# First loads and splits in parts, zero products beside them, and VectorE's small steps in shorter strings: a two-layer kernel on one core

## The reference

```python
x = layernorm(x + L0_attn(x))   # linear attention, 16 heads of 128, 4 key/value heads
x = layernorm(x + L0_ffn(x))    # a gate picks one of 8 small updates per token
x = layernorm(x + L1_attn(x))   # softmax attention, 16 heads of 16
x = layernorm(x + L1_ffn(x))    # 8 experts, the two best per token

# L0_attn
sq, sk = elu(q) + 1, elu(k) + 1
kv = einsum('bhsd,bhse->bhde', sk, v)
out = einsum('bhsd,bhde->bhse', sq, kv) / (einsum('bhsd,bhd->bhs', sq, sk.sum(2)) + 1e-6)
# L0_ffn: gate = sigmoid(slope * (score - center)); argmax and max over the 8
# L1_ffn: scores = softmax(x @ G); top 2 of 8 weigh the experts
```

## Time and profile before

| what | value |
|---|---|
| time, median of 3 runs | 769.73 us (767.15 to 775.13) |
| the profiled execution's own time | 768.48 us |
| its span, first to last instruction | 766.7 us |
| mean granted TensorE clock | 0.934 |
| PE busy | 700.3 us, 91% |
| DVE busy | 509.6 us, 66% |
| ACT busy | 405.0 us, 53% |
| POOL busy | 110.4 us, 14% |

### The profile page before, as it was taken

The page is one execution under the profiler, slowest core; times in us unless marked ns, Lnnn a source line. Parts: engine busy times, 40 slices in busy tenths (PEclk is TensorE's granted clock), DMA queues, the critical chain, the costliest instruction groups (busy, mean ns, idle before and its releaser), DMA issues.

```text
span 766.7 us, 11317 instructions
## 1 busy us (share of the span) xinstructions
PE 700.3 (91%) x4028; PEld 481.7 (63%) x4028; DVE 509.6 (66%) x1125; ACT 405.0 (53%) x746; POOL 110.4 (14%) x107
## 2 busy tenths in 40 slices
PE   4799999999999999997899988999999899999674
PEld 3677988798878887895344534555565455455463
DVE  2657755775577666767778777868779786772343
ACT  2376536643674377453037745764647565656222
POOL 0401321132203322243002010200001000000000
PEclk9899999999999999998559969998999999999868
DMA  8300000010000020008704810373006700000000
GB/s 340 128 0 2 28 1 1 2 31 14 0 0 0 11 77 1 4 1 103 100 2 55 98 15 2 44 90 36 2 2 77 89 30 2 1 2 29 28 1 27
DMA packets 13596, 28.30 MB, mean 37 GB/s; under 512 B 2596, under 2 KB 3436, under 8 KB 13036
## 3 DMA queue, kind: packets, MB, share of 16 engines
q1 hardware_dynamic: 13548, 27.68, 19.6%
HBM read 12.60 MB, written 2.10 MB: 19 GB/s over the span
## 4 chain that ended last, share of the span: by engine, by line
PE 74%; DVE 14%; ACT 5%; issue 3%; DMA 2%; POOL 1%; ACTq 0%; DVEq 0%; POOLq 0%
PE bank_y L391 11%; PE bank_q L332 10%; PE bank_st L1134 9%; PE bank_c L1147 6%; PE bank_a L296 6%; DVE nmax L1699 5%; PE side L1206 4%; PE bank_a L362 3%; PE side L1082 3%; PE bank_s L1113 3%; PE side L1237 2%; PE bank_a L308 2%; PE bank_n L347 2%; PE bank_q L374 2%; PE side L1166 2%
## 5 line engine op out<-in xcount | busy, mean ns | idle before, releaser
L1699 DVE TENSOR_REDUCE nmax<-bank_s 128x1 f32<-128x512 f32 x256 | 164.5, 684 | 62.8 <-PE bank_s L1113 62.2
L1460 ACT ACTIVATE shared<-bank_st 128x512 f32<-128x512 f32 x256 | 139.2, 596 | 78.4 <-PE bank_st L1134 77.8
L1113 PE MATMUL bank_s<-ks,qs 48*128 48x512 f32 x256 | 117.7, 524 | 10.4 <-DVE nmax L1699 8.6
L1134 PE MATMUL bank_st<-qs,ks 50*128 50x512 f32 x256 | 104.8, 480 | 5.6 <-ACT shared L1460 5.4
L578 DVE SCALAR_TENSOR_TENSOR sq<-bank_q,bq,eq 128x512 f32<-128x512 f32 x64 | 47.6, 743 | 52.2 <-ACT eq L473 52.2
L1134 PEld LDWEIGHTS bank_st<-qs,ks 50*128 50x128 f32 x256 | 42.6, 197 | 54.6 <-issue 28.0
L391 PE MATMUL bank_y<-m_hi,s_lo 128*128 128x256 f32 x256 | 73.3, 286 | 3.2 <-POOL s_lo L248 3.1
L1147 PE MATMUL bank_c<-shared,v 128*32 128x512 f32 x512 | 73.5, 648 | 0.9 <-ACT shared L1460 0.9
L391 PE MATMUL bank_y<-m_lo,s_hi 128*128 128x256 f32 x256 | 72.1, 282 | 0.0
L391 PE MATMUL bank_y<-m_hi,s_hi 128*128 128x256 f32 x256 | 72.1, 282 | 0.0
L248 POOL TENSOR_TENSOR s_lo<-sq,s_hi 128x512 fp32r<-128x512 f32 x32 | 42.8, 1339 | 189.5 <-ACT s_hi L478 189.5
(11 more groups left out here) (251 smaller groups left out, 1329.8 us busy)
## 6 DMA issues: line engine op xcount, KB each, us to landing
qs<-qk_hi SPq DMA_DIRECT2D x16, 256.0 KB, 5.9
ks<-qk_hi SPq DMA_DIRECT2D x16, 256.0 KB, 10.2
xT<-in_xT SPq DMA_DIRECT2D x4, 512.0 KB, 5.3
sq<-in_wqT SPq DMA_DIRECT2D x2, 1024.0 KB, 9.2
wo<-in_woT SPq DMA_DIRECT2D x1, 2048.0 KB, 12.9
xs<-in_x SPq DMA_DIRECT2D x1, 2048.0 KB, 17.8
qs<-qk_lo SPq DMA_DIRECT2D x8, 256.0 KB, 7.9
ks<-qk_lo SPq DMA_DIRECT2D x8, 256.0 KB, 10.9
```

The lines of the kernel that those rows point to most:

```text
L1113: pe.matmul(bank_s[u % 2][:, :], qs[part, b % 2, slot, t * P:(t + 1) * P], ks[part, b % 2, slot, :], start=True, stop=True).then_inc(s_don ...
L1134: pe.matmul(bank_st[u % 2][:, :], ks[part, b % 2, slot, kt * P:(kt + 1) * P], qs[part, b % 2, slot, :], start=True, stop=True).then_inc(st ...
L1460: act.activation(probs[:, u % SLOTS, :], bank_st[u % 2][:, :], ACT.Exp, scale=SCALE1).then_inc(p_ready, 1)
L1699: dve.tensor_reduce(nmax[:, g, t, j:j + 1], bank_s[u % 2][:, :], AX.X, ALU.max, negate=True).then_inc(max_ready, 1)
```

## The change

It has three parts.

1. **Head.** SP loads `xT` first, then key weights and value weights as two DMAs of 512 KB, the biases, and the query weights cut by heads (two DMAs of 1 MB with eight heads each) instead of by inputs. DVE copies the key weights' `hi` itself (two copies of 128 x 512) and takes rests piece by piece; ACT splits `xT` first, then the values' weights. PE runs `WARM_UP` = 5 products of zeros (`ksel`, 256 columns each, nobody reads the result) while the loads run, and then `first_keys_values`, tile 0's products in an order that needs the rests last. `split_queries` stands behind key tiles 0 and 1 on ACT, behind tile 1's values and behind the last key on DVE. Batch 0 takes three queries ahead of its state, as the other batches do.
2. **Layer 1's small steps.** `gate_scores` becomes three pieces at n = 21, 22 and 23, `gate_pick` two at n = 25 and 27; the routing becomes `route_rel` 15, `route_scores` 17, `route_first` 18, `route_less` 19 and `route_second` 20, with `turn_logits` on PE at n = 14 and `route_exp` on ACT at 16; `gate_exp` moves from 22 to 24, `turn_hm` and `hmT_out` from 28 to 30, and they use `bank_t` instead of `side[0]`. The statistics of batch 3's residual in b = 0 move from n = 11 and 12 to n = 28 and 29. The number of steps and their work stay.
3. **Single places.** In the middle DVE takes `qk_rest(0, 1)` ahead of `normalize_x1(1)`. On ACT `normalize(4, B - 2)` moves from the end of the last body behind `context_out(B - 1, 3)`.

The diff, cut to its core:

```diff
         def sync(sp):
-            sp.dma_start(stage[:, 0, :], a["wkvT0"]).then_inc(stage_in[0], 16)
             sp.dma_start(xT[:, :, :], a["xT"][:, 0]).then_inc(xT_in, 16)
-            sp.dma_start(ones[:, :], a["ones"]).then_inc(ones_in, 16)
+            sp.dma_start(raw_k, a["wkT0"]).then_inc(wk_in, 16)
+            sp.dma_start(raw_v, a["wvT0"]).then_inc(wv_in, 16)
...
-            for k in range(KD):
-                sp.dma_start(stage[:, 1 + k, :], a["wqT0"][:, k]).then_inc(stage_in[1 + k], 16)
+            for i in range(2):
+                sp.dma_start(raw_q[:, :, half_heads(i)], a["wqT0"][:, :, half_heads(i)]).then_inc(wq_in[i], 16)
+            sp.dma_start(ones[:, :], a["ones"]).then_inc(ones_in, 16)
...
+            def first_keys_values():
+                tok = slice(0, P)
+                for part, (bank, done) in enumerate(((bank_a[0], k_done), (bank_a[1], v_done))):
+                    cols = slice(part * 512, (part + 1) * 512)
+                    for k in range(KD):
+                        pe.wait_ge(xT_hi_ready, k + 1)
+                        if part == 0:
+                            pe.wait_ge(wk_hi_ready, k + 1)
+                        else:
+                            pe.wait_ge(wv_hi_ready, 1)
+                        pe.matmul(bank[:, :], xT_hi[:, k, tok], wkv_hi[:, k, cols], start=k == 0, stop=False)
+                    for k in range(KD):
+                        pe.wait_ge(xT_lo_ready, k + 1)
+                        pe.matmul(bank[:, :], xT_lo[:, k, tok], wkv_hi[:, k, cols], start=False, stop=False)
...
                 for t in range(NT):
+                    if first and t == 0:
+                        continue
                     key_value(b, t)
                     beside("key", t)
-                if first:
-                    state(b)
-                    pe.wait_ge(w_hi_ready, len(W_STAGES))
-                    pe.wait_ge(w_lo_ready, len(W_STAGES))
                 for n in range(3):
+                    if first and n != 1:
+                        pe.wait_ge(wq_lo_ready, 1 + n // 2)
                     query(b, n)
                     beside("query", n)
-                if not first:
-                    state(b)
+                state(b)
...
+            pe.wait_ge(ksel_zeroed, 1)
+            zeros = ksel[:, :, :, :].rearrange("p g j c -> p (g j c)")
+            for i in range(WARM_UP):
+                pe.matmul(bank_n[:, 0:TH], zeros[:, 0:P], zeros[:, 0:TH], start=True, stop=True)
+            first_keys_values()
             body(0, True)
...
-                    if t == 3 and not last:
-                        split_weights(1)
+                    if t == 1 and not last:
+                        split_queries(0)
...
-            split_weights(0)
+            dve.wait_ge(wk_in, 16)
+            for k in range(KD):
+                dve.tensor_copy(wkv_hi[:, k, 0:512], raw_k[:, k, :]).then_inc(wk_hi_ready, 1)
             for k in range(KD):
                 split_x(0, k)
+                split_keys(k)
+            split_values()
             dve.wait_ge(kv_bias_in, 32)
...
+        def update_home(b):
+            return 0 if b < 2 else "t"
...
-                    if n == 28 and most:
+                    if n == 30 and most:
                         turn_hm(b + 2)
...
-                    if b == 0 and n in (5, 11):
-                        residual_stats(2 + n // 11, range(NT))
+                    if b == 0 and n in (5, 28):
+                        residual_stats(2 + n // 28, range(NT))
...
-                    if n == (16 if more else 15) and back:
+                    if n == 15 and back:
                         route_rel(b - 1)
+                    if n == (17 if more else 16) and back:
+                        route_scores(b - 1)
                     if n == (18 if more else 16) and back:
                         route_first(b - 1)
-                    if n == (19 if more else 17) and back:
+                    if n == (19 if more else 16) and back:
+                        route_less(b - 1)
+                    if n == (20 if more else 17) and back:
                         route_second(b - 1)
-                    if n == 20 and most:
-                        gate_scores(b + 2)
...
+                    if n == 21 and most:
+                        gate_distances(b + 2)
+                    if n == 22 and most:
+                        gate_inverse(b + 2)
                     if n == 23 and most:
-                        gate_pick(b + 2)
+                        gate_scores(b + 2)
+                    if n == 25 and most:
+                        gate_largest(b + 2)
+                    if n == 27 and most:
+                        gate_pick(b + 2)
...
             qk_rest(0, 0)
+            qk_rest(0, 1)
             normalize_x1(1)
-            qk_rest(0, 1)
...
-                    if n == 31 and not more:
-                        normalize(4, b - 1, xk[:, (b - 1) % 2])
...
             context_out(B - 1, 3)
+            normalize(4, B - 2, xk[:, (B - 2) % 2])
             normalize(3, B - 1, xk[:, (B - 1) % 2])
```

More of the change, by code:

```diff
@@ L1305, in body @@
                         route(b - 1)
-                    if n == (15 if more else 14) and back:
+                    if n == 14 and back:
                         turn_logits(b - 1)
@@ L1524, in body @@
                         x1T_out(b + 2, n - 16)
-                    if n == (17 if more else 15) and back:
+                    if n == (16 if more else 15) and back:
                         route_exp(b - 1)
@@ L1532, in body @@
                         tanh(b - 1, (n - e) // 2)
-                    if n == 22 and most:
+                    if n == 24 and most:
                         gate_exp(b + 2)
```

140 lines of the change are left out of this document (86 added, 54 removed).

## The result

| | before | after |
|---|---|---|
| time, median of 20 runs each | 770.49 us (766.71 to 779.62) | 760.0 us (755.03 to 768.9) |
| ratio | 1 | 0.9846 (95% interval 0.9816 to 0.9877) |
| span of the profiled execution | 766.7 us | 754.1 us |
| mean granted clock of it | 0.934 | 0.943 |
| PE busy | 700.3 us, 91% | 701.9 us, 93% |

The change makes the kernel faster by 1.5%. The forecast was 749.7 us, its range 744 to 760: the direction is right, the size is about half of what I said (10.5 us by the medians, 12.6 by the two profiled spans, instead of 20.0). The median lies on the very edge of the range; what holds it is the width that the range had for the rivals, not the forecast.

The account below looks back on a forecast made before the run. TensorE was busy 91% of the span; its idle time and low-clock time were to be gained. 9.0 + 9.5 + 0 + 1.8 = 20.3, less 0.3, took the span from 766.7 to 746.7; plus 3.0, 749.7 us, range 744 to 760.

Parts of the forecast that it names:

- the rivals: Other outcomes: clock falls again 0.21; VectorE the bound or head lost in part 0.17; both 0.07; slower 0.02.
- Head, 9.0 forecast: Start of the kernel: query 3 starts between 31.3 and 33.5 instead of 41.6, 9.0 us saved, bounds 5.5 to 10.3.
- the second split: Head: DVE's second split of the query weights, 2.2 us behind the last `sk`, ends at 25.7; query 2 waits for it.
- Strings, 9.5 forecast: Layer 1's strings of small DVE steps: 4.5, 2.8 and 2.2 us saved in b = 0, 1 and 2; bounds 0 to 13.4.
- by the row: Layer 1: the low level came behind a stall of 1.81 us, so the strings are worth the low stretches too.
- 0.3 for new small waits: Last term of the sum: 0.3 us taken off 20.3, leaving 20.0 saved.
- the clock falls all the same: Rival, layer 1: low stretches may need no long stall; strings give only their stalls, 4.1 us; 14.6 saved, 755.1; chance 0.21.
- about 2.0 more for DVE: Layer 1, b = 0: moved statistics (1.39) and their merge at n = 28 and 29 raise DVE's load from 25.3 to 27.3 us.
- Middle, 0 forecast: Middle: earlier `qk_rest(0, 1)` gains nothing since the DMA engines are full; 0, bounds 1 us either way.
- Tail, 1.8 forecast: End: ACT copies the last context at 716.1 instead of 717.96, 1.8 us saved, all on the chain.
- up to 2.5 more: End: additional saving, up to 2.5 us, if PE then stays at the high level.
- What was to show it: Signs in the profile: first product, tile 1, state, query 3, `nmax` waits, clock, last copy; wrong if lead under 5 us.

Follow-up runs that it names:

- key sums late: Changed kernel with GpSimd's second and third key sum of batch 0 behind VectorE's second query-weight split; query 3 at 33.21 instead of 34.2, one execution.
- the state first: Changed kernel with batch 0's state ahead of query 2 instead of behind it; ratio to before 0.9762 (0.9694 to 0.983).
- the tail's profile: Profile of the kernel before with one edit, normalize(4, B - 2) behind context_out(B - 1, 3); ratio 0.9936, a long execution with mean granted clock 0.925.
- the long strings: Layer 1's small steps as before the change: profiles of the kernel before, of it with only the head changed, and of it with only the tail changed.
- The strings alone: Kernel before with only layer 1's shorter strings, batch 3's statistics at n = 28 and 29 included; ratio 1.0001 (0.9964 to 1.0038).
- the second profile: Profile of the changed kernel run once more, unchanged; ratio to before 0.9784 (0.9698 to 0.9869).
- fillers: Changed kernel with 18 more products of 128x512 in the tail, result unread: 14 behind the last out_project, 4 ahead of the routing product; ratio 0.9872.
- the kernel with the head alone: Kernel before with only the change's head: loads, splits, zero products, tile 0's order, three queries ahead of the state; ratio 0.9885 (0.9823 to 0.9948).

## Why the prediction was right in direction and half in size

**Head, 9.0 forecast, 7.2 measured (7.0 and 6.8 in two more profiles).** Query 3 stood at 41.44 before, not 41.6. The order of the steps was right, each term a little short. VectorE started at 6.45 instead of 5.8: I had taken the landing of the old first megabyte, but the key weights landed 5.2 us after an issue at 1.2. Its copies took 0.38 each (I had 0.5). The first product came at 7.0 instead of 6.3. Tile 0 ended at 12.8 instead of 11.7: I had three slow products, and nearly all were slow. In two other profiles it ended at 11.9, so part of this differs between executions. The stop ahead of tile 3 was 1.39, as said (1.4). The mis-sized term is the second split: 2.2 in the sum, 3.38 measured, since GpSimd's key sums run beside it; together with its later start it held query 2 until 28.34 instead of 25.7. State and key sums took 4.4 us (3.3 + 0.8 forecast). Query 3 came at 34.2, past the 31.3 to 33.5 given. The last run of the head (key sums late) gives back 1.0 of it, the state first 2.3.

**Strings, 9.5 forecast.** Two halves of unequal worth.
- The three stretches of the strings were sized well. Over all profiles they are 8.9 us shorter (4.8, 2.4 and 1.7 for 4.5, 2.8 and 2.2; the 4.8 is without the half-steps from n = 28 on, where the statistics take 2 to 3 us back), and at the high level n = 17 to the end of b = 0 takes 28.7 us (I had 29.5, with the statistics). The low stretches behind the stalls did go with the stalls, "by the row", as the forecast had it.
- *The step that failed* is the sum's last term: outside these stretches it put nothing but "0.3 for new small waits". New low stretches came, behind waits that had stood in the kernel before and had been followed by the high level there: b = 0, n = 12 (1.01 us), b = 1, n = 4 (0.76), b = 3, n = 8 (0.53 and 0.35). The last of these is in the tail's profile too, which has the long strings; low time in the first half of b = 1 is in eight of the eleven profiles with the short strings and in none of the three with the long ones, and costs 3.1 us in the mean. The strings alone leave the mean low time where it was (108.6 against 107.9 us) and give 1.0001 +- 0.0037.
- The rival "the clock falls all the same" came nearest. With the head's 7.2 in it, its sum is 7.2 + 4.1 + 1.8 - 0.3 = 12.8, a span of 753.9 where the profile has 754.1. That they meet is luck: in that profile the strings' stretches gave 10.4 us, three other places took back 5.7, and the tail gave 0.6 for 1.8. Its reason, that a low stretch may need no long stall, is what the second profile shows at 440 to 447. Its median would be 756.9; the measured 760.0 is 3 us more. Of these the statistics can be 2.7 by their place, but the executions at equal low time don't bear that out, and the rest stays open.
- "In b = 0 about 2.0 more for DVE" was a sum over 30 us, and it fell into one gap: 1.39 us in one piece ahead of a maximum stopped TensorE for 0.98. I had argued from this very mechanism for the strings, and added the statistics as an average.

Of the rule quoted in the forecast from the Trainium skill, "TensorE: Matmul & The Clock Gate", section "Why this matters for your kernels" (gaps above about 3 us are to be avoided): its forecast for the strings, the stalls alone, came closer than mine in the whole. Its reason doesn't hold here: in the three profiles with the long strings the level fell behind each stall of 1.06 to 1.82 us, and elsewhere behind waits of 0.32 to 1.01 us, while in other executions it stayed high behind waits of the same length.

**Middle, 0 forecast.** Right: 7.22 at query 3, 7.04 at b = 0, n = 0. TensorE's wait for the key rows' DMA went from 1.0 to 0.5 us, without an effect on the lead.

**Tail, 1.8 forecast.** ACT copies the context 0.02 us behind its product, and TensorE's wait went from 2.47 us to 0.72, which is the 1.8:

```profile
704.22 0.60 ACT L1515 ACTIVATE ctT<-bank_c 128x512 f32<-128x512 f32 x1 [1.19 <-PE bank_c L1192]
704.71 2.06 ACT L1457 ACTIVATE xk<-xk,ln_shift,ln_rstd 128x256 f32<-128x256 f32 x4
```

Alone the edit gives 0.9936 (0.9895 to 0.9978), 1.7 to 8.1 us; at equal low time 0.6 +- 0.7. In the whole's first profile only 0.6 reached the end: out_project's first eight products took 1.97 us at the high level instead of 3.60, but behind n = 31 of b = 3 there are 27.9 us at the low level where there were 25.5. By place the term looks too small: from n = 31 of b = 3 to the end the nine with the edit and no fillers took 48.6 to 52.7 us (mean 50.4), the four without it 53.3 to 54.0 (mean 53.6). That is 3.2 us, within the 1.8 and "up to 2.5 more" of the forecast. But at equal low time even 1.8 is outside the bounds, so whether the idle time taken away reached the end, or the executions with the edit had less low time by chance, stays open.

**What was to show it.** Held: the copy within 0.2 us; at n = 18 to 28 of b = 0, 1 and 2 the longest wait for `nmax` is 0.15 us and, in the first profile, the granted clock 1.00 (in the second, 440 to 447 is at 0.52); the lead at query 3 above 5 us. Late: first product 7.0 for 6.3, tile 1 12.8 for 11.7, state 29.8 for 27, query 3 34.2 for 32. n = 17 to the end of b = 0 took 31.4 us, just under the 32 that I had set, and 32.7 in the second profile, just over it. And low stretches stood where none were, which I had named as what would make it wrong. I had watched the places of the strings, where nearly all came true; the loss lay beside them.

## What to carry to other kernels

A low stretch of TensorE's clock that stands behind a stall in every profile can be that stall's and still not be won: here it went with the stall, and others came where the edit had changed next to nothing. So credit an edit with the idle time it removes, and with a low stretch only once the whole kernel's low time has fallen over many executions. Two profiles can't show this; lengths stretch by stretch over ten or more can, and so can a fit of time against low time. Spread what you move: a lump of 1.4 us on an engine that has gaps in the mean still stops the engine that waits for its next result. When a wait can't be shortened, look whether the work behind it can stand ahead of it: the state ahead of query 2 was worth 2.3 us and one `if`.

## What the runs showed of the hardware

- In the three profiles with long strings of small VectorE steps 13.7 us at the low level followed a stall of 1.81 us, and 3.4 us one of 1.26; with the stalls gone, both were shorter or gone in ten of eleven profiles, and the first half of b = 1 took 47.0 to 52.9 us in eight of them instead of 45.4.
- The time at the 1.2 GHz level differs by 46 us between executions of the same changed kernel (74 to 120 us), and each microsecond of it costs 0.35 us here.
- The same wait (0.77 us, same instructions to 0.02 us) is followed by the high level in the changed kernel's first profile and by a context of nearly twice the length (1.94 us for 1.07) in its second.
- VectorE's subtraction of 128 x 2048 took 2.28 us alone and 3.38 beside GpSimd's additions, which took 1.35 each alone and 2.48 beside it.
- Products of tile 0 come 0.43 us apart in the kernel with the head alone, nearly twice the later 0.235, although the granted clock of that stretch reads 1.00. In the changed kernel's profile the same stretch reads 0.57. So a 1.00 near the start has to be checked against the distance of the products.

```profile
9.00:13.00 4.00, 4.00 (x10) 2.92 (x10) 2.38 (x4) 1.56 (x3) 0.00 (x0) 1.00 1.02 411
```
